# A graph attention layer in two fp32r parts: its preparation rebuilt around plain fp32 and a spread through device memory

## What is computed

```
h  = h @ W1 + b1
e  = leaky_relu((h @ a1)[:, None] + (h @ a2)[None, :] + b2, 0.2)
attention = softmax(where(adj > 0, e, -1e12), axis=1)
out = x + elu(attention @ h)
```

## Time and profile before

| | us |
|---|---|
| median of 3 runs | 437.63 |
| profiled execution | 437.48 |
| its span | 435.7 |
| PE busy | 412.5 (95%) |
| DVE busy | 377.1 (87%) |
| ACT busy | 315.9 (73%) |

### The profile page before, as it was taken

One profiled execution on the slowest core, in us unless ns is written; L12 is line 12 of the kernel. 1 busy time (PEld: TensorE's weight loads), 2 busy tenths in 40 slices (PEclk: granted clock), 3 DMA queues, 4 the chain that ended last, 5 costly groups with the idle time before them and its releaser, 6 DMA issues.

```text
span 435.7 us, 8648 instructions
## 1 busy us (share of the span) xinstructions
PE 412.5 (95%) x3399; PEld 409.1 (94%) x3399; DVE 377.1 (87%) x404; ACT 315.9 (73%) x312; POOL 23.0 (5%) x94
## 2 busy tenths in 40 slices
PE   0689979999999999999999999999999999999995
PEld 0688979999999999999999999999999999999995
DVE  3999899999999389999996299999991799999925
ACT  2678899999996298957763798859562989586512
POOL 2333200000000000000000000000000000000003
PEclk9999999999999999999999999999999999999999
DMA  8940015556555725638478155647477256476202
GB/s 271 385 178 1 0 45 211 193 213 211 193 193 194 289 93 205 235 145 261 173 254 308 68 193 200 249 152 263 154 265 259 73 219 213 174 243 238 98 0 98
DMA packets 22360, 80.68 MB, mean 185 GB/s; under 512 B 1472, under 2 KB 14016, under 8 KB 14144
## 3 DMA queue, kind: packets, MB, share of 16 engines
q1 hardware_dynamic: 21920, 79.70, 52.1%
q10 hardware_dynamic: 416, 0.66, 0.5%
HBM read 76.15 MB, written 4.19 MB: 184 GB/s over the span
## 4 chain that ended last, share of the span: by engine, by line
PE 88%; DVE 7%; ACT 2%; DMA 2%; issue 0%; SPq 0%; DVEq 0%; ACTq 0%
PE ps L604 51%; PE ps L606 25%; PE ps L622 2%; PE ps L623 2%; PE ps L624 2%; DVE stats L664 2%; DMA x_s<-x 2%; DVE hnT_lo L691 1%; PE ps L531 1%; DVE h_raw L700 1%; PE ps L533 1%; PE ps L532 1%; DVE xn L681 1%; PE ps L580 1%; PE ps L519 1%; ACT h_raw L439 1%
## 5 line engine op out<-in xcount | busy, mean ns | idle before, releaser
L604 PE MATMUL ps<-hp_hi,w_hi 128*128 (+1 forms) x944 | 229.8, 282 | 0.9 <-ACT w_hi L391 0.9
L606 PE MATMUL ps<-hp_lo,w_hi 128*128 (+1 forms) x944 | 229.7, 282 | 0.0
L738 DVE SCALAR_TENSOR_TENSOR adj_s<-R,p,adj_s 128x1024 f32<-128x1024 f32 x128 | 158.1, 1275 | 31.7 <-ACT adj_s L383 31.7
L604 PEld LDWEIGHTS ps<-hp_hi,w_hi 128*128 128x128 f32 x944 | 178.3, 189 | 1.2 <-ACT w_hi L391 1.1
L606 PEld LDWEIGHTS ps<-hp_lo,w_hi 128*128 128x128 f32 x944 | 178.1, 189 | 0.0
L748 DVE SCALAR_TENSOR_TENSOR w_lo<-adj_s,w_hi 128x2048 fp32r<-128x2048 f32 x64 | 146.0, 2282 | 0.4 <-ACT w_hi L391 0.3
L391 ACT ACTIVATE w_hi<-adj_s 128x2048 fp32r<-128x2048 f32 x64 | 122.4, 1912 | 29.8 <-DVE adj_s L738 29.5
L383 ACT ACTIVATE adj_s<-adj_s 128x2048 f32<-128x2048 int32 x64 | 122.3, 1912 | 23.2 <-DMA adj_s<-adj_t 23.0
L604 PE MATMUL ps<-hp_hi,w_lo 128*128 (+1 forms) x944 | 123.1, 283 | 0.6 <-DVE w_lo L748 0.6
L604 PEld LDWEIGHTS ps<-hp_hi,w_lo 128*128 128x128 f32 x944 | 117.4, 189 | 0.8 <-DVE w_lo L748 0.8
L455 ACT ACTIVATE y<-ps 128x258 f32<-128x258 f32 x24 | 9.3, 387 | 27.9 <-PE ps L624 27.9
(11 more groups left out here) (90 smaller groups left out, 270.2 us busy)
## 6 DMA issues: line engine op xcount, KB each, us to landing
adj_s<-adj_t SPq DMA_DIRECT2D x64, 1024.0 KB, 4.8
x_s<-x SPq DMA_DIRECT2D x8, 512.0 KB, 10.4
o_s<-x SPq DMA_DIRECT2D x3, 1024.0 KB, 7.5
out<-o_s SPq DMA_DIRECT2D x6, 512.0 KB, 6.8
adj_s<-x SPq DMA_DIRECT2D x1, 1024.0 KB, 5.3
out<-adj_s SPq DMA_DIRECT2D x8, 128.0 KB, 1.7
vec<-vectors ACTq DMA_DIRECT2D x1, 384.5 KB, 6.4
W1x<-W ACTq DMA_DIRECT2D x1, 256.0 KB, 4.3
```

Source lines behind the costliest of these rows:

```text
L604: last = pe.matmul(acc, block_w, hh, start=False, stop=False)
L606: pe.matmul(acc, block_w, hl, start=False, stop=False)
L738: last = dve.scalar_tensor_tensor(sgn, R[:, ds(ic * CW, CW)], p[:, ds(source(r, c) + s, 1)], sgn, ALU.max, ALU.mult)
```

## The change

- `project` uses plain fp32 operands, hnT and W1x: 8 matmuls a group. hnT_lo, `low_T`, W_hi, W_lo and `split_weights` go.
- R: the column cr is transposed (`turn_r`), Exp is taken of 8 or 24 rows (`exp_r`), SP stores the rows to device memory and loads them back into all partitions (`spread` on SP), in two parts of 1024 and 3072 nodes. `repeat_s1`, the old `spread`, `keep_s` and `exp_R` go.
- ScalarE normalises three of four tiles, into four buffers (XN); for groups 0 and 1 VectorE's bn_aggr takes the place of GpSimd's moments, and the split stays at two and two. The relus' PSUM banks alternate (T0).
- TensorE runs `keep_warm` before its first transposes; W1 and the vectors are loaded from SP's queue behind the first x group.
- The last group's scores go from PSUM straight into s2 and cr, and the maximum is taken of s2 ahead of the last `keep_h`.
- The tiny sums are added in `last_pairs`, at a chunk's end (one `add_tiny` a bank, for 4 chunks as before); h_tiny is made inside chunk 0 (`tiny`). The first tile's first matmul opens the bank.

The diff, cut to its core; longer removed runs, which stand in the code above, are left out:

```diff
-NORM_ACT = 2
+NORM_ACT = 3
+AGG = 2
+WARM = 14
+XN = 4
+R_CUT = CW // P
+R_PART = ((0, R_CUT), (R_CUT, TILES))
...
-EARLY = 6 * GT
+EARLY = 4 * GT
...
-        xn = over("xn", [P, 2, GT, F], fp32, w_hi, 2 * 2 * CW * 4)
-        hnT = over("hnT", [P, 2, KC, GT * P], fp32r, w_hi, 3 * 2 * CW * 4)
-        hnT_lo = over("hnT_lo", [P, 2, KC, GT * P], fp32r, w_hi, 2 * CW * 4)
+        xn = over("xn", [P, XN, GT, F], fp32, w_hi, 2 * CW * 4)
+        hnT = over("hnT", [P, 2, KC, GT * P], fp32, w_hi, 3 * 2 * CW * 4)
...
+        T0 = (0, 6)
+        RB = (1, 6)
+        GB = 7
...
+            load_nodes(0)
+            sp.dma_start(W1x[:, :, 0:F], W1.rearrange("(c p) f -> p c f", p=P)).then_inc(w_in, 16)
+            sp.dma_start(vec[:, :], vectors.partition_broadcast(P)).then_inc(vec_in, 16)
+            for g in range(1, GROUPS):
                 load_nodes(g)
-                if g == 3:
-                    load_adj(0, 0)
+            load_adj(0, 0)
             for s in range(1, SLOTS):
                 load_adj(s, s)
+            def spread(k):
+                a, b = R_PART[k]
+                tiles = slice(a, b)
+                sp.wait_ge(r_ready, k + 1)
+                sp.dma_start(r_rows[tiles, :], r_row[k][:, :]).then_inc(r_out, 16)
+                sp.wait_ge(r_out, (k + 1) * 16)
+                sp.dma_start(R[:, a * P:b * P],
+                             r_rows[tiles, :].rearrange("t p -> (t p)").partition_broadcast(P)).then_inc(R_in, 16)
+            spread(0)
+            spread(1)
...
+            pool.memset(ones64[:, :].bitcast(fp32), 1.0 / 64).then_inc(h_sum_set, 1)
+            pool.memset(h_sum[:, F:F + 1], float(N)).then_inc(h_sum_set, 1)
+            pool.memset(h_sum[:, F + 1:HW], 0.0).then_inc(h_sum_set, 1)
...
-            for g in range(4):
+            for g in range(AGG, 5):
                 moments(g)
             pool.wait_ge(g3_ready, 1)
-            for g in range(GROUPS):
-                if g + 4 < GROUPS:
-                    moments(g + 4)
+            for g in range(GROUPS - 1):
+                if g + 5 < GROUPS:
+                    moments(g + 5)
                 exponents(g)
+            tiles = slice((GROUPS - 1) * GT, GROUPS * GT)
+            pool.wait_ge(s2_kept, 1)
+            pool.tensor_scalar(cp[:, tiles], s2[:, tiles], -(1 - SLOPE), TOP, ALU.mult, ALU.min).then_inc(c_ready, 1)
...
+            def root_agg(g):
+                act.wait_ge(agg_ready, GT * (g + 1))
+                act.activation(std[:, g * GT:(g + 1) * GT], agg[:, g, :, 1], ACT.Sqrt, bias=eps[:, 0:1]).then_inc(std_ready, 1)
...
+            def exp_r(k):
+                act.wait_ge(rT_ready, k + 1)
+                act.activation(r_row[k][:, :], ps[0:R_PART[k][1] - R_PART[k][0], RB[k], 0:P], ACT.Exp).then_inc(r_ready, 1)
...
-            root(0)
+            root_agg(0)
             normalise(0)
-            root(1)
+            relu_T(0)
+            root_agg(1)
             normalise(1)
-            relu_T(0)
-            sign(0, 0, 0)
-            for g in range(GROUPS):
+            relu_T(1)
+            root(2)
+            normalise(2)
+            root(3)
+            relu_T(2)
+            normalise(3)
+            root(4)
+            for g in range(2, GROUPS):
+                if g + 2 < GROUPS:
+                    normalise(g + 2)
+                if g == 5:
+                    exp_r(0)
+                    act.wait_ge(c_ready, EARLY // GT)
+                    act.activation(p[:, 0:EARLY], cp[:, 0:EARLY], ACT.Exp).then_inc(p_ready, 1)
                 if g + 1 < GROUPS:
                     relu_T(g + 1)
...
                 if g + 3 < GROUPS:
                     root(g + 3)
-                if g >= 1:
-                    repeat_s1(g - 1)
+                if g == 3:
+                    sign(0, 0, 0)
                 if g == 6:
...
+                    sign(0, 0, 1)
                     high(0, 0, 0)
...
+            exp_r(1)
...
-                    if r is FIRST_ROUND and c == 2 and not last:
-                        exp_R(ic + 1)
...
-            keep_s(GROUPS - 2)
-            keep_s(GROUPS - 1)
-            act.wait_ge(s_kept, GROUPS)
+            act.wait_ge(c_ready, GROUPS)
+            act.activation(p[:, EARLY:TILES], cp[:, EARLY:TILES], ACT.Exp).then_inc(p_ready, 1)
+            act.wait_ge(ones_col, 2)
...
+            def keep_warm(n):
+                for _ in range(n):
+                    pe.matmul(ps[:, H0 + GT - 1, 0:P], ones[:, :], ones[:, :], start=True, stop=True)
+                for cols in (P // 4, P // 2, P):
+                    for _ in range(6):
+                        pe.matmul(ps[:, H0 + GT - 1, 0:cols], ones64[:, :], ones64[:, 0:cols], start=True, stop=True)
...
-                        pe.matmul(acc, hnT[:, u, kc, node], W_hi[:, kc, :], start=kc == 0, stop=False)
-                        pe.matmul(acc, hnT[:, u, kc, node], W_lo[:, kc, :], start=False, stop=False)
-                        last = pe.matmul(acc, hnT_lo[:, u, kc, node], W_hi[:, kc, :], start=False, stop=kc == KC - 1)
+                        last = pe.matmul(acc, hnT[:, g % 2, kc, node], W1x[:, kc, :], start=kc == 0, stop=kc == KC - 1)
...
+            def turn_r(k):
+                a, b = R_PART[k]
+                pe.transpose(ps[0:b - a, RB[k], 0:P], cr[:, a:b], ident[:, :]).then_inc(rT_ready, 1)
...
+            pe.wait_ge(h_sum_set, 1)
+            keep_warm(WARM)
+            transposes(0)
+            pe.wait_ge(w1x_ready, 1)
+            project(0)
+            transposes(1)
+            project(1)
+            transposes(2)
+            for g in range(2, GROUPS):
+                if g + 1 < GROUPS:
+                    transposes(g + 1)
+                if g == 4:
+                    pe.wait_ge(c_ready, R_CUT // GT)
+                    pe.wait_ge(hn_ready, (g + 1) * KC)
+                    turn_r(0)
+                project(g)
+                if g == 4:
+                    pe.wait_ge(r_ready, 1)
...
+            pe.wait_ge(cr_end, 1)
+            turn_r(1)
...
+            def add_tiny(ib):
+                pe.matmul(ps[:, ib, 0:HW], ones64[:, :], h_tiny[:, :], start=False, stop=False)
+            def first_tile():
+                pe.wait_ge(hi_ready, 1)
+                pe.wait_ge(hp_tile, 1)
+                pe.wait_ge(hsum_kept, 1)
+                pe.wait_ge(r_ready, 2)
+                for ib in range(BANKS):
+                    if ib == H0:
+                        pe.wait_ge(h_kept, 2 * GROUPS)
+                    pe.matmul(ps[:, ib, 0:HW], w_hi[:, 0, 0, ib * P:(ib + 1) * P], hp_hi[:, 0, :], start=True, stop=False)
+                pe.wait_ge(hp_first, 1)
+                for ib in range(BANKS):
+                    pe.matmul(ps[:, ib, 0:HW], w_hi[:, 0, 0, ib * P:(ib + 1) * P], hp_lo[:, 0, :], start=False, stop=False)
...
+                            fresh = begin and part == 0 and s == 0
+                            if fresh:
+                                pe.wait_ge(evacuated, (ic - 1) * BANKS + ib + 1)
+                            last = pe.matmul(acc, block_w, hh, start=fresh, stop=False)
...
+            def aggregate(g):
+                for t in range(GT):
+                    dve.bn_aggr(agg[:, g, t, :], stats[:, g, t, :]).then_inc(agg_ready, 1)
...
             statistics(0)
-            statistics(1)
+            aggregate(0)
             invert(0)
             normalise(0)
             weights()
+            statistics(1)
+            aggregate(1)
             invert(1)
             normalise(1)
-            split_weights()
-            low_T(0)
             statistics(2)
+            keep_h(0)
+            statistics(3)
+            invert(2)
+            normalise(2)
+            statistics(4)
+            invert(3)
+            normalise(3)
+            keep_h(1)
             scalars()
-            statistics(3)
-            for g in range(GROUPS):
-                if 0 < g < GROUPS - 2:
+            for g in range(2, GROUPS - 1):
+                if g + 2 < GROUPS:
                     invert(g + 2)
...
                     normalise(g + 2)
...
+                if g + 3 < GROUPS:
+                    statistics(g + 3)
+                keep_h(g)
+                if g == 5:
                     dve.wait_ge(p_ready, 1)
-                    dve.wait_ge(R_ready, 1)
+                    dve.wait_ge(R_in, 16)
                     mask(0, 0, 0)
-                keep_h(g)
-
+            dve.wait_ge(hn_ready, GROUPS * KC)
+            link(dve.reduce_sum(hsum[:, :], hs[:, :, :], AX.X))
+            for kc in range(KC):
+                last = dve.tensor_scalar(hsrep[:, kc, :], ones[:, :], hsum[:, kc:kc + 1], None, ALU.mult)
+            last.then_inc(hsrep_ready, 1)
+            end = slice((GROUPS - 1) * GT, TILES)
+            early = slice(0, (GROUPS - 1) * GT)
+            dve.wait_ge(c_ready, GROUPS - 1)
+            dve.memset(h_raw[:, early, F], 1.0)
+            dve.memset(h_raw[:, early, F + 1], 0.0).then_inc(ones_col, 1)
```

(58 more changed lines are left out.)

179 lines of the change are left out of this document (38 added, 141 removed).

## The result

The changed kernel takes **440.36 us**, the median of 6 runs (439.44 to 442.31), against 437.62 for the kernel before (6 runs, 437.43 to 437.81): the ratio is 1.0071, with a 95% interval of 1.0045 to 1.0098. It is 0.7% slower, and outside the predicted range. The profiled execution took 442.31 us, the slowest of the six, so its rows show about 2 us more than the median has.

A forecast was written before the change was run, and what follows sets the result against it. PE bounds the dense main loop, so edits count by moving pair 1's start from 65.68. Front -6.2, projections +6.3, end -0.75 and -0.8 sum to -1.4 us: 437.48 becomes 436.1 us, range 434.0 to 439.5.

The forecast's parts named there:

- my sum: Whole kernel: -6.2 + 6.3 - 0.75 - 0.8 = -1.4 us, pair 1 starting at 64.3, time 436.1 us; chance 0.45.
- project(0) starts at 10.8: Preparation's first part: the first projection starts at 10.8 us, not 17.0, so earlier by 6.2 us.
- My bound of 10: TensorE's warm-up: ends at 10 us with small matmuls of 0.12 and a late clock rise; 8.7 was taken.
- 1.2, 2.6, 4.3: PE's waits in us: for relu_T(1) before project(1), for tiles before transposes(3), for r_ready after project(4).
- a rival of chance 0.25: Clock lost in PE's waits: work behind runs at half rate, middle cost 2.6 us, time 438.7; chance 0.25.
- perhaps: The clock rival's place: the 4.3 us wait after project(4), perhaps also the 2.6 us one.
- nothing shows a fall at all: Argument against the clock rival: the trace before showed no clock fall; longest idle time left at high level was 1.59 us.
- The rule that I had quoted: TensorE's clock: a wait of a few microseconds between bursts sends the engine back to half its clock.
- 4.36 us a group: Projection stage: PE's own work per group, 3.48 us of projection and 0.88 of transposes, becomes the bound.
- the 2.5 that I gave: End chain: u starts about 2.5 us after the last projection, 3.2 before; gain 0.75.
- 32 before and after: nothing: Main loop: each chunk's 8 tiny sums move from its begin to its end, 32 before and after, costing nothing.
- R through device memory: R's store and broadcast load, from 40.95 to 46.15 us, cost nothing, with 0.4 us of slack.

The follow-up runs named there:

- experiment 1: The changed kernel with 10 matmuls of ones ahead of transposes(3) and 18 ahead of the wait for r_ready: 437.46 us, 0.9996 of before.
- experiment 3: The changed kernel with a shorter warm-up, WARM = 8 for 14: 441.12 us, 1.0091 of before.
- experiment 5: The kernel before with the plain fp32 projection alone, without low_T, W_hi, W_lo and split_weights: 437.68 us, 1.0009 of before.
- experiment 6: experiment 2 with 7 matmuls of ones in the wait after project(4): 433.50 us, 0.9909 of before.
- experiment 2: The changed kernel with normalise(3) ahead of relu_T(2) and the Exp of R's first rows ahead of normalise(7): 434.39 us, 0.993 of before.
- experiment 7: experiment 6 with chunk 0's tiny sums between its first and second pair and 5 fills in the end chain: 433.00 us, 0.9899 of before.
- experiment 12: experiment 7 with R's first exponent later, the sum of h's replicas ahead of the first mask, W1 and vectors on ScalarE's queue: 431.27 us, 0.9853 of before.
- experiment 4: The changed kernel with keep_warm taken out: 442.55 us, 1.0123 of before.
- experiment 11: The changed kernel with normalise(3) ahead of relu_T(2) alone: 437.95 us, 1.0008 of before.
- experiment 8: experiment 7 with W1 and the vectors loaded from ScalarE's queue and WARM = 8: 435.01 us, 0.9944 of before.

## Why the prediction was wrong

The profiled execution stands 442.31 - 436.1 = 6.2 us over my sum: 5.1 lie ahead of pair 1, 1.1 in the loop. The median stands 4.3 us over it; experiment 1, which keeps the clock up in the two waits, takes 2.9 of them away.

- **The front** ("project(0) starts at 10.8"): 11.98, 1.2 late. x was used at 4.31 and the normalised tiles stood at 8.06, as I had them. The warm-up ended at 9.9 and not at 8.7: nearly all of its first 28 records ran at the lower level (6.21 us; 28 at 0.217 would take 6.3). My bound of 10 held, my value did not. vec came at 8.69 for 7.2, and cost nothing here, since the warm-up was later; with the shorter one of experiment 3 the weights made of it were what TensorE waited for.
- **The waits** ("1.2, 2.6, 4.3"): 0.92, 2.45, 4.28. The chain of rows for each was right to 0.3 us; with them, 0.45 less than I had.
- **The clock: the step that failed.** I let it keep its level in the waits and put its loss into a rival of chance 0.25, with a middle of 2.6. From begin to begin, against the same work in experiment 1, transposes(3) lost 0.53 and project(2) 1.14, transposes(6) 0.84 and project(5) 1.54: 4.05 in this execution. The second wait's 2.38 are near the rival's middle of 2.6; the first wait's 1.67 I had only as a "perhaps". Over all executions experiment 1 puts it at 2.9. I argued that "nothing shows a fall at all"; but nothing could, since the longest idle time in that trace once the clock was up was 1.59 us, and the change made waits outside all that the trace had shown. The rule that I had quoted beside the rival (the Trainium skill, "TensorE: Matmul & The Clock Gate", "HAM oscillation — how this bites in real kernels") foretold this; the trace agrees behind the longer wait, with 0.50 from 43 to 47 us, and shows the same behind the 2.45 us one, with 0.50 at 26. It should have been the likeliest case, and would have given 438.7 or more.
- **The projections** ("4.36 us a group"): right in a run of groups, 36.02 - 31.55 = 4.47 with the turn of 0.11. But where a wait follows, the burst counts to its end and not to the next start (3.65 us for a projection and not 3.49), and the transposes behind one take 1.09 us for 1.03, at full clock too: without waits and clock the stage took 35.1 us where I had 34.1. 1.0 more. My reading that VectorE gave the pace before, and TensorE waited for it, held up to about 41 us; from 42 to 50 TensorE was the bound already, at 4.20 us a group (experiment 5). There the plain fp32 projection had nothing to gain, and cost 0.16 us a group.
- **The end**: u began 1.95 us behind the last projection, for the 2.5 that I gave, and pair 1 8.4 behind u's end, as I had it: 0.65 less in all. The clock fell in this short chain as well (0.52 from 64 to 66), so pair 0 took 7.5 us for 5.8; pair 1's high part came at 69.37 in any case. Experiment 6 bears this out: its pair 0 took 6.0 us, and its pair 1 began at 60.60 where experiment 2, with a slow pair 0, has 60.62.
- **The tiny sums** ("32 before and after: nothing"): wrong by 1.0. The count is the same, but before, 8 of them lay ahead of pair 1, in time in which PE waited for ScalarE anyway; now all lie in the dense loop, where a matmul costs its 0.120 us: 8 x 0.12 = 0.96. The last matmul starts at 436.01, the spacing is the same, and experiment 7 gave 0.8 of it back.
- **R through device memory**: cost nothing, as said. Issued at 43.93, the load landed 3.3 us behind its own issue at 45.16, 4.6 us for the 5.2 that I gave, and the mask at 51.56 did not wait.

```profile
R<-r_rows SPq DMA_DIRECT2D x1, 1536.0 KB, 6.3
...
R<-r_rows SPq DMA_DIRECT2D x1, 512.0 KB, 3.3
```

Together 64.3 + 1.2 - 0.45 + 4.05 + 1.0 - 0.65 = 69.45 for pair 1, where the trace has 69.41. Even with the clock kept (experiment 1) the change is worth nothing. The large rework of the preparation gave its gain at the front, and lost it to two waits in ScalarE's order, 6.7 us long, once TensorE had become the bound: each of them counts whole, and takes the clock with it. Experiments 2, 6 and 12 show that the parts are worth having once the order is mended.

The step of the prediction that failed is thus the one by which TensorE kept its clock through the waits, priced at nothing in the sum; it cost 4.05 us in the profiled execution and 2.9 over all. The late front (1.2), the tiny sums put at nothing (1.0) and the projections without waits (1.0 under) came on top, and the shorter end (0.65) and waits (0.45) took back as much as one of them.

Open: why the waits of 2.04 to 2.45 us took the clock in some executions and not in others; and whether R's first rows could be turned in a bank of their own while the projections go on, which was not tried.

## What to carry to other kernels

When an edit relieves the engine that is the bound, ask first how far behind the next one stands, and then walk the queue of that next engine: every wait in it that was slack is now path, and the cure is often to move one instruction of its partner ahead of another. A wait longer than any that the trace shows is priced with the loss of the clock in the main case, not in a rival, and a shorter one is not safe for being shorter; if it can't be shortened, a few matmuls on constants in it cost nothing here. And instructions that are moved in equal number are not moved at no cost: count how many of them go from slack into the dense loop.

## What the runs showed of the hardware

The granted clock fell to half with the waits of 4.27 to 4.29 us in each of the profiled kernels that had one (the changed one, experiments 3, 4 and 11). In two of them it fell in the wait itself, and in two only behind it: in experiment 11 the transposes after the wait still took 1.09 us, and the clock read 0.50 between 41 and 43 us, in the middle of the next projection, though TensorE was busy by then. For waits of 2.04 to 2.45 us it fell in two profiled executions (the changed kernel, experiment 4) and held in two (experiments 2 and 3). It also fell behind shorter ones: behind the 1.20 us of experiment 8, and in pair 0 of the changed kernel and of experiments 1, 2, 3, 4 and 11, where the longest wait of the end chain ahead of it is 1.36 or 1.37 us. In experiment 6 it held through the same 1.36 us, and in the kernel before through 1.59. So the length of the longest wait alone does not tell whether the clock falls. The time from the first matmul of a burst to the full level differed from execution to execution of the same instructions: the 28 records of the warm-up took 4.91 us in one kernel (experiment 6) and 6.27 in another (experiment 12). The clock's column reads full speed from 2 to 8 us, although these records come at the lower level: at the start of a kernel the records' durations are to be read, not the column. A plain fp32 matmul shows as two records, and costs 0.436 us at 258 columns at the full level (3.49 for 8) where an fp32r one costs 0.120: as much as 3.6 of them.
